# Query, key and value projections of a self-attention as three float32r products of split operands

## The chip, the core and the metric

One core of a Trainium2 chip runs the whole program. The metric is the device time of one execution in microseconds (us), the median of several. The engines have queues of their own and wait for each other by semaphores only: TensorE (PE in the rows; PEld is its weight load), VectorE (DVE), ScalarE (ACT), GpSimd (POOL), SyncE (SP, which issues the transfers).

## The reference

Inputs are x (2 x 1024 tokens, 256 features) and a context of 2 x 77 tokens. Two layers follow. The part that matters here is the start of the first one:

```python
h = layernorm(x)
ca = attention(q=h @ cq_w + cq_b, k=ctx @ ck_w + ck_b, v=ctx @ cv_w + cv_b)   # 16 heads of 16, 77 keys
x1 = norm(ca @ co_w + co_b + h) * co_g + co_be
q, k, v = x1 @ sq_w + sq_b, x1 @ sk_w + sk_b, x1 @ sv_w + sv_b                 # the change is here
sa = attention(q, k, v)                                                        # 1024 keys
...                                       # output norm, GELU block, experts, second attention, ternary block
```

## The kernel before

The 2048 tokens are 16 tiles of 128 (t), four tiles a block (k). The program has three parts. Part A (0 to about 215 us) does the first attention and the projections of the second. Part B (to about 565 us) is the self-attention over 32 batch-heads. Part C is everything else.

Part A is a list of steps, `ORDER_A`, written out by hand. Each engine walks the same list and does its share of each step, in that order and in no other: an instruction that waits holds up all later steps of its engine. Steps carry a tile, block or other number (S.13). They are:

- LS: moments of x on VectorE, reciprocal root on GpSimd (function `root`, L1919 and L1920). LN0: normalised tile (VectorE L1493), transposed (TensorE L861), copied by ScalarE (L1276). QP: queries of a block (TensorE L855).
- S: scores on TensorE (L908, L915), maximum and subtraction on VectorE (L1530, L1531). E: exponential on ScalarE. T: transposes of the probabilities in four groups, ScalarE copies each (L1298). PV: values (TensorE L931, ScalarE L1304). OT: transposes (TensorE L861 to OUT), divided on VectorE (L1538, L1539). CT: transposes again, ScalarE copies. PJ: output projection on TensorE (L855), residual addition and moments on VectorE (L1522, L1486, L1487), root on GpSimd. PN: normalisation of the projected tile on VectorE (L1493, L1496, L1497). RA: a bias addition on GpSimd (L1929).
- LT: transposes of the tile that PN wrote (TensorE L861, ScalarE L1276), into `xTb`. QK: query and key projections of a block, four groups `e` of 128 features by 512 tokens (TensorE L855). For each group ScalarE makes two copies (L1356, L1357), VectorE their difference (L1634), and SyncE stores both parts. SV: value projection of a tile (TensorE L855), bias addition on VectorE (L1640).
- MX: score maxima of the first two heads of part B (TensorE L962, VectorE L1555). MT, LH: maxima to rows, load of first heads. UT, GG, FL: a low-rank weight product for part C. FL is 4 products with 16 rows contracted, copied by ScalarE (L1343). KW, VV, MK, KB, V0, VW, CX, CK, ZS: preparation.

TensorE writes to rings of PSUM banks. `TR` has two banks, emptied by ScalarE; `OUT` has two banks, emptied by VectorE (OT, PJ, SV); the scores have their own four. A step that takes a bank waits until the user two before it in the same ring has been emptied:

```python
def out_bank(tl):
    bank = tl.slot(out_full, 2)
    tl.next(out_full)
    v = tl.back(out_full, 2)
    pe.wait_ge(out_done.sem, v)
    return OUT[:, bank, :]
```

All products of the projections are in float32; the trace shows each as two MATMUL instructions. Part B and the last stage of part C use float32r, one instruction a product. Part B begins on TensorE when every bank of part A is emptied, FL's among them. At the same point SyncE issues the loads of four weight arrays, and soon after the rows of head 1's maxima.

Of the kernel before, what the change touches and what calls it, by code (L numbers as in the profile page):

```python
# [23 lines left out]
F32 = mybir.dt.float32  # L24
# [9 lines left out]
KD = D // 128  # L34
# [57 lines left out]
    "LT": dict(tr=1),  # L92
    "RA": dict(res=1),
# [268 lines left out]
def build(nc, A, out):  # L362
    ctx = ExitStack()
    with ctx:
# [39 lines left out]
        projT = sb("projT", [128, MF, D], F32R)  # L404
        so, wq, wo = (sb(n, [128, KD, D]) for n in ("so", "wq", "wo"))
# [28 lines left out]
        xTb, xTs = xT3[:, 0], xT3[:, 1]  # L434

# [130 lines left out]
        placed = Signal(sem("slots_placed"), **count("place"))  # L566
        h_ready = Signal(sem("high_parts_ready"), **count("top"))
# [1513 lines left out]
```

## Time and profile before

| | us |
|---|---|
| median of 3 runs | 1096.81 |
| lowest, highest | 1096.51, 1098.58 |
| profiled execution, first to last instruction | 1094.8 |
| mean granted TensorE clock in it | 0.975 |
| TensorE matmul busy | 1019.2 |
| VectorE busy | 782.0 |
| ScalarE busy | 607.7 |
| GpSimd busy | 331.8 |

For the profiled execution the span is what the profile gives; its own time lies above the span by what comes before the first and after the last instruction. Matmuls are pipelined and their ends are modelled, so starts and distances of starts say more than durations. The granted clock is 1.00 at 2.4 GHz and 0.50 at 1.2 GHz.

### The profile page before, as it was taken

To read this page: it belongs to the slowest core of one execution; us is meant where nothing else is said; L and a number is where in the kernel's file an instruction comes from. 1 tells how busy PE (TensorE), PEld (TensorE's weight loads), DVE (VectorE), ACT (ScalarE), POOL (GpSimd) and SP (SyncE) were. 2 spreads that over 40 slices of the span, in tenths; PEclk is the share of its full clock that TensorE was granted. 3 is DMA by queue.
4 is the path that set the end of the run, shared out by engine and by line. 5 is a ranking of instruction groups with operands and counts; after the bars stand their busy time and mean duration, and the time that the engine had idled before them with its cause. 6 is when DMAs were issued, how large, how long until landed. Compare 5 with 4: busy or idle time off the path is not lost.

```text
span 1094.8 us, 20748 instructions
## 1 busy us (share of the span) xinstructions
PE 1019.2 (93%) x7648; PEld 601.0 (55%) x7648; DVE 782.0 (71%) x1337; ACT 607.7 (56%) x1191; POOL 331.8 (30%) x724
## 2 busy tenths in 40 slices
PE   5999989999999999999988898989898999999998
PEld 3675666433333333333344665648677676576865
DVE  4786577689999999999723747546536756887565
ACT  2665554478888888888853123131222456556543
POOL 3422111001010343344103334373366433530000
PEclk9999999889999999999998997999999999999999
DMA  7302221451221212212125100021344301100000
GB/s 213 70 16 88 87 68 66 144 188 44 75 71 48 70 49 69 79 45 70 47 67 191 34 15 10 20 77 44 101 155 132 100 31 49 44 25 1 16 18 26
DMA packets 97578, 75.67 MB, mean 69 GB/s; under 512 B 49806, under 2 KB 87483, under 8 KB 97223
## 3 DMA queue, kind: packets, MB, share of 16 engines
q1 hardware_dynamic: 94407, 65.95, 20.0%
q0 software_dynamic: 3072, 8.39, 2.4%
q8 instruction: 63, 1.03, 0.4%
q14 instruction: 36, 0.29, 0.1%
HBM read 42.94 MB, written 30.93 MB: 67 GB/s over the span
## 4 chain that ended last, share of the span: by engine, by line
PE 65%; DVE 10%; DMA 8%; issue 5%; POOL 4%; ACT 4%; SPq 3%; POOLq 0%; DVEq 0%; ACTq 0%
PE OUT L855 15%; PE TR L855 14%; PE OUT L1090 9%; PE TR L861 8%; PE TR L1079 7%; DMA head_q<-MT 7%; PE OUT L1079 3%; PE TR L931 3%; PE SCR L915 2%; POOL dispatched L2038 2%; SPq L697 2%; ACT PTS L1298 2%; PE SCR L908 2%; DVE small L1486 1%; PE OUT L861 1%
## 5 line engine op out<-in xcount | busy, mean ns | idle before, releaser
L1555 DVE TENSOR_REDUCE small<-SCR 128x1 f32<-128x1024 f32 x256 | 308.5, 1223 | 26.2 <-PE SCR L962 20.3
L1396 ACT ACTIVATE shared<-TR 128x512 f32<-128x512 f32 x352 | 200.1, 597 | 38.8 <-PE TR L1079 30.7
L962 PE MATMUL SCR<-head_k,head_q 48*128 48x512 f32 x512 | 193.9, 456 | 2.7 <-DVE P L1531 2.7
L1090 PE MATMUL OUT<-shared,HM 128*32 128x256 f32 x2048 | 165.3, 394 | 1.2 <-ACT shared L1396 0.4
L1079 PE MATMUL TR<-head_q,head_k 51*128 51x512 f32 x352 | 149.7, 463 | 0.9 <-issue 0.6
L1919 POOL TENSOR_SCALAR small<-small 128x1 f32<-128x1 f32 x112 | 27.7, 247 | 346.7 <-DVE small L1487 344.5
L855 PE MATMUL TR<-xT,fifo 128*128 128x512 f32 x224 | 105.8, 629 | 1.1 <-ACT xT L1276 1.0
L1396 ACT ACTIVATE shared<-OUT 128x512 f32<-128x512 f32 x160 | 95.8, 599 | 19.3 <-PE OUT L1079 17.6
L1079 PEld LDWEIGHTS TR<-head_q,head_k 51*128 51x128 f32 x352 | 60.6, 186 | 76.4 <-ACT shared L1396 56.5
L1276 ACT ACTIVATE xT<-TR 128x256 f32<-128x256 f32 x96 | 35.4, 381 | 111.5 <-PE TR L861 108.6
L1090 PEld LDWEIGHTS OUT<-shared,HM 128*32 128x32 f32 x2048 | 41.4, 108 | 93.1 <-ACT shared L1396 57.6
L1298 ACT ACTIVATE PTS<-TR 96x512 f32<-96x512 f32 x128 | 69.6, 589 | 38.5 <-PE TR L861 37.8
L1936 POOL CAST small<-small 128x8 bf16<-128x8 f32 x32 | 6.1, 190 | 256.5 <-DVE small L1555 256.5
L962 PEld LDWEIGHTS SCR<-head_k,head_q 48*128 48x128 f32 x512 | 79.1, 187 | 7.0 <-DVE P L1531 3.0
L861 PE MATMUL TR<-identf,P 128*96 128x128 f32 x512 | 71.1, 281 | 7.7 <-ACT PTS L1298 7.4
L855 PEld LDWEIGHTS TR<-xT,fifo 128*128 128x128 f32 x224 | 44.4, 203 | 55.3 <-issue 49.1
L1079 PE MATMUL OUT<-head_q,head_k 51*128 51x512 f32 x160 | 70.2, 438 | 4.7 <-DMA head_q<-MT 4.2
L1920 POOL TENSOR_TENSOR small<-small 128x1 f32<-128x1 f32 x112 | 67.1, 599 | 9.3
L861 PEld LDWEIGHTS TR<-identf,P 128*96 128x96 f32 x512 | 52.8, 127 | 23.4 <-ACT PTS L1298 16.3
L1530 DVE TENSOR_REDUCE small<-SCR 128x16 f32<-128x1232 f32 (+1 forms) x32 | 48.7, 1522 | 20.2 <-PE SCR L915 19.9
L855 PE MATMUL OUT<-fifo,shared 128*128 128x256 f32 x256 | 58.2, 382 | 2.0 <-ACT shared L1426 1.6
L855 PE MATMUL TR<-xT,fcT 128*128 128x512 f32 x128 | 56.2, 595 | 1.0 <-ACT RR L1440 1.0
(241 smaller groups left out, 1860.3 us busy)
## 6 DMA issues: line engine op xcount, KB each, us to landing
pieces<-pieces SPq DMA_DIRECT2D x16, 512.0 KB, 2.7
HM<-dispatched SPq DMA_DIRECT2D x46, 128.0 KB
expert_out<-HM SPq DMA_DIRECT2D x46, 128.0 KB
dispatched<-HB SPq DMA_DIRECT2D x6, 768.0 KB, 4.0
head_q<-pieces SPq DMA_DIRECT2D x32, 128.0 KB
head_k<-pieces SPq DMA_DIRECT2D x32, 128.0 KB
shared<-in_L_ffn_w SPq DMA_DIRECT2D x4, 1024.0 KB, 12.0
x<-TOK SPq DMA_DIRECT2D x16, 128.0 KB, 1.7
```

Source lines behind the costliest of these rows:

```text
L855: ins = nc.tensor.matmul(dst, l, r, start=(n == 0), stop=(n == len(pairs) - 1))
L861: ins = nc.tensor.transpose(dst[0:m, n * width:n * width + p], s, ident[0:p, 0:p])
L931: ins = nc.tensor.matmul(bank[32 * g:32 * g + 32, c * 128:(c + 1) * 128], VSW[0:KP, h, :], PTS[0:KP, place, :], start=True, stop=True)
L962: ins = nc.tensor.matmul(SQ[kt % 2][:, hf, :], QX[n % 2][rows, kt * 128:(kt + 1) * 128], KX[n % 2][rows, hf * 512:(hf + 1) * 512], start=T ...
L1079: nc.tensor.matmul(bank, KX[n % 2][rows, kt * 128:(kt + 1) * 128], QX[n % 2][rows, hf * 512:(hf + 1) * 512], start=True, stop=True)\
L1090: ins = nc.tensor.matmul(PV[32 * g:32 * g + 32, 0:256], VH[:, n % 2, kt, :], PTB[:, kt % 2, g * 256:(g + 1) * 256], start=(kt == 0), stop= ...
L1276: nc.scalar.activation(dst[:, :, c:c + 128], bank[:, 0:256].rearrange("p (k n) -> p k n", k=KD), ACT.Copy)\
L1298: nc.scalar.activation(PTS[0:KP, 4 * g:4 * g + 4, :], bank[0:KP].rearrange("p (h n) -> p h n", h=4), ACT.Copy)\
L1396: nc.scalar.activation(PTB[:, kt % 2, hf * 512:(hf + 1) * 512], ring_bank("t_scores", n, kt, hf), ACT.Exp, scale=DH ** -0.5).then_inc(st_d ...
L1530: chain(nc.vector.tensor_reduce(mx, v, AX, ALU.max))
L1555: nc.vector.tensor_reduce(nm[:, n % 2, kt:kt + 1], SQ[kt % 2].rearrange("p h n -> p (h n)"), AX, ALU.max, negate=True).then_inc(sq_done.se ...
L1920: nc.gpsimd.tensor_tensor(rstd[:, r:r + 1], ve[:, r:r + 1], minus_half, ALU.pow)\
```

## The change

The input of the self-attention projections, x1, and the three weights are each split in a high part (rounded to float32r) and a low part (the rest, as float32r). A product becomes three: high by high, high by low, low by high, accumulated in one bank. QK has six float32r products a group in place of two float32 ones, and SV likewise.

Step LT becomes LA: the transposes go to an OUT bank, ScalarE copies it into `XAH` (high part), and VectorE subtracts that from the same bank into `XAL` and frees the bank. QK and SV wait for VectorE's part of LA. A new step WS on GpSimd splits the weights once, before QP.1. FL moves from between MX.1.6 and MX.1.7 to the very end of the list. PN of a tile waits for LA's transposes of the tile two before it, where it waited for LT's copy; VectorE's own part of LA stands ahead of it in the list.

```diff
     "LT": dict(tr=1),
+    "LA": dict(out=1, ahi=1),
+    "WS": dict(),
...
-QP.1 PV.2 LN0.8 LS.10 LS.9 LS.12 S.4 LS.11 T.3 E.4 OT.2 PJ.1 PV.3 S.5 CT.2 OT.3 T.4 PJ.2 LT.0 PV.4 RA.6 RA.3 E.5 PN.1
-CT.3 LS.13 S.6 OT.4 T.5 PN.2 PJ.3 LT.1 E.6 PV.5 CT.4 S.7 T.6 OT.5 SV.1 E.7 LT.2 PV.6 RA.4 LN0.10 PN.3 PJ.4 CT.5 OT.6
-T.7 LS.14 LN0.11 LN0.9 RA.5 SV.0 RA.7 LT.3 PV.7 LN0.12 RA.8 RA.10 VW.1 PJ.5 CT.6 RA.12 QP.2 LN0.13 SV.2 PN.5 S.8 QK.0
-S.9 E.8 OT.7 PN.4 SV.3 T.8 S.10 E.9 PV.8 PJ.6 LT.4 CT.7 OT.8 T.9 E.10 PJ.7 SV.4 CT.8 PV.9 LN0.14 PN.6 PJ.8 LT.5 LT.6
-PN.7 OT.9 T.10 RA.9 SV.5 LT.7 PV.10 LN0.15 SV.7 CT.9 QK.1 S.11 LH.0 QP.3 PJ.9 E.11 OT.10 S.12 T.11 SV.6 E.12 PN.8 S.13
-PN.9 CT.10 PV.11 LT.8 PJ.10 OT.11 T.12 S.14 CT.11 RA.11 E.13 PN.10 PV.12 PJ.11 RA.13 T.13 E.14 OT.12 S.15 CT.12 MX.0.0
-LT.10 LH.1 E.15 PV.13 PJ.12 LT.9 MX.0.1 SV.10 RA.14 MX.0.2 T.14 OT.13 MX.0.3 MX.0.4 PV.14 CT.13 MX.0.5 PN.11 RA.15
-SV.9 MX.0.6 T.15 OT.14 MX.0.7 PJ.13 LT.11 PN.12 PV.15 PN.13 MX.1.0 CT.14 MX.1.1 OT.15 PJ.14 QK.2 SV.11 CT.15 SV.8
-LT.12 PN.14 MT PJ.15 LT.13 MX.1.2 UT PN.15 SV.12 LT.14 SV.13 MX.1.3 MX.1.4 LT.15 SV.14 QK.3 MX.1.5 MX.1.6 FL MX.1.7
-SV.15
...
+WS QP.1 PV.2 LN0.8 LS.10 LS.9 LS.12 S.4 LS.11 T.3 E.4 OT.2 PJ.1 PV.3 S.5 CT.2 OT.3 T.4 PJ.2 LA.0 PV.4 RA.6 RA.3 E.5
+PN.1 CT.3 LS.13 S.6 OT.4 T.5 PN.2 PJ.3 LA.1 E.6 PV.5 CT.4 S.7 T.6 OT.5 SV.1 E.7 LA.2 PV.6 RA.4 LN0.10 PN.3 PJ.4 CT.5
+OT.6 T.7 LS.14 LN0.11 LN0.9 RA.5 SV.0 RA.7 LA.3 PV.7 LN0.12 RA.8 RA.10 VW.1 PJ.5 CT.6 RA.12 QP.2 LN0.13 SV.2 PN.5 S.8
+QK.0 S.9 E.8 OT.7 PN.4 SV.3 T.8 S.10 E.9 PV.8 PJ.6 LA.4 CT.7 OT.8 T.9 E.10 PJ.7 SV.4 CT.8 PV.9 LN0.14 PN.6 PJ.8 LA.5
+LA.6 PN.7 OT.9 T.10 RA.9 SV.5 LA.7 PV.10 LN0.15 SV.7 CT.9 QK.1 S.11 LH.0 QP.3 PJ.9 E.11 OT.10 S.12 T.11 SV.6 E.12 PN.8
+S.13 PN.9 CT.10 PV.11 LA.8 PJ.10 OT.11 T.12 S.14 CT.11 RA.11 E.13 PN.10 PV.12 PJ.11 RA.13 T.13 E.14 OT.12 S.15 CT.12
+MX.0.0 LA.10 LH.1 E.15 PV.13 PJ.12 LA.9 MX.0.1 SV.10 RA.14 MX.0.2 T.14 OT.13 MX.0.3 MX.0.4 PV.14 CT.13 MX.0.5 PN.11
+RA.15 SV.9 MX.0.6 T.15 OT.14 MX.0.7 PJ.13 LA.11 PN.12 PV.15 PN.13 MX.1.0 CT.14 MX.1.1 OT.15 PJ.14 QK.2 SV.11 CT.15
+SV.8 LA.12 PN.14 MT PJ.15 LA.13 MX.1.2 UT PN.15 SV.12 LA.14 SV.13 MX.1.3 MX.1.4 LA.15 SV.14 QK.3 MX.1.5 MX.1.6 MX.1.7
+SV.15 FL
...
-            before(("LT", t), ("PN", t + 2))
+            before((last, t), ("PN", t + 2))
...
-    attention_order(before, range(T))
+    attention_order(before, range(T), "LA")
+    before(("WS",), ("LA", 0))
     for t in range(T):
         k = t // BT
         for u in range((k - 1) * BT, k * BT):
             if u >= 0:
-                before(("SV", u), ("LT", t))
+                before(("SV", u), ("LA", t))
         if k >= 1:
-            before(("QK", k - 1), ("LT", t))
+            before(("QK", k - 1), ("LA", t))
...
+        WH = over("self_weights_high", [128, 3, KD, D], F32R, "projT")
+        WL = over("self_weights_low", [128, 3, KD, D], F32R, "fifo", 1024)
...
+        XAH, XAL = (over(f"self_in_{n}", [128, KD, N], F32R, "xT3", KD * N * j) for j, n in enumerate(("high", "low")))
...
+            def self_input(t):
+                pe.wait_ge(tok_ready.sem, tl.after(tok_ready, "PN", t))
+                bank = out_bank(tl)
+                transposes(bank, [TOK[:, t % 2, k * 128:(k + 1) * 128] for k in range(KD)]).then_inc(out_full.sem, 1)
+
             def self_qk(k):
-                at.block_copied("LT", k)
-                for w in (sq, sk):
-                    for m in range(KD):
-                        at.feature_major(w, xTb, m)
+                pe.wait_ge(out_done.sem, tl.after_block(out_done, "LA", k))
+                pe.wait_ge(ws_ready, 1)
+                for e in range(2 * KD):
+                    j, c = e // KD, slice(e % KD * 128, e % KD * 128 + 128)
+                    bank = tr_bank(tl)
+                    product(bank, [(w[:, j, f, c], x[:, f, :]) for f in range(KD)
+                                   for w, x in ((WH, XAH), (WH, XAL), (WL, XAH))]).then_inc(tr_full.sem, 1)
 
             def self_values(t):
-                at.copied("LT", t)
-                at.token_major(xTb, sv, t, range(KD))
+                pe.wait_ge(out_done.sem, tl.after(out_done, "LA", t))
+                pe.wait_ge(ws_ready, 1)
+                bank = out_bank(tl)
+                c = slice(t % BT * 128, t % BT * 128 + 128)
+                product(bank[:, 0:D], [(x[:, f, c], w[:, 2, f, :]) for f in range(KD)
+                                       for x, w in ((XAH, WH), (XAH, WL), (XAL, WH))]).then_inc(out_full.sem, 1)
...
+            def self_input(t):
+                bank = OUT[:, tl.slot(out_full, 2), :]
+                act.wait_ge(out_full.sem, tl.next(out_full))
+                c = t % BT * 128
+                nc.scalar.activation(XAH[:, :, c:c + 128], bank[:, 0:256].rearrange("p (k n) -> p k n", k=KD), ACT.Copy)\
+                    .then_inc(xa_ready.sem, 1)
...
-                    left(tl, "LT", t - 2)
+                    dve.wait_ge(out_full.sem, tl.after(out_full, "LA", t - 2))
                 normalised(tl, chain, ("PJ", t), HB[:, t % 2, :], TOK[:, t % 2, :], affine="co")\
                     .then_inc(tok_ready.sem, 1)
+
+            def self_input(t):
+
+                bank = filled(tl)
+                dve.wait_ge(xa_ready.sem, tl.next(xa_ready))
+                c = t % BT * 128
+                signal_out(tl, nc.vector.tensor_tensor(
+                    XAL[:, :, c:c + 128], bank[:, 0:256].rearrange("p (k n) -> p k n", k=KD),
+                    XAH[:, :, c:c + 128].bitcast(F32), ALU.subtract))
...
+            def self_weights():
+
+                pool.wait_ge(d_aw, 16 * 4)
+                for j, w in enumerate((sq, sk, sv)):
+                    chain(nc.gpsimd.tensor_copy(WH[:, j, :, :], w))
+                    ins = nc.gpsimd.tensor_tensor(WL[:, j, :, :], w, WH[:, j, :, :].bitcast(F32), ALU.subtract)
+                ins.then_inc(ws_ready, 1)
```

## Rows read from the trace of the kernel before

**Rows 1.** Page, part 1: busy us (share of the span) and instructions.
```profile
PE 1019.2 (93%) x7648; PEld 601.0 (55%) x7648; DVE 782.0 (71%) x1337; ACT 607.7 (56%) x1191; POOL 331.8 (30%) x724
```

**Rows 2.** Windows view, 50 to 200 us: length, busy of each engine, clock, DMA.
```profile
50.00:200.00 150.00, 142.86 (x1253) 97.64 (x1252) 112.76 (x208) 83.75 (x149) 28.90 (x62) 0.99 0.19 68
```

**Rows 3.** Chain of work in order of time: start, us, what.
```profile
91.91 0.87 PE OUT L855 x4
...
124.03 6.87 PE TR L855 x16
...
197.62 1.13 PE SCR L962 x4
...
222.68 6.46 DMA head_q<-MT
...
232.24 0.23 PE TR L1079
```

**Rows 4.** Timeline of PE, output stage, float32r: start, us, engine, line.
```profile
1087.05 0.28 PE L855 MATMUL OUT<-projT,hidL 128*128 128x256 f32 x1
1087.17 0.28 PE L855 MATMUL OUT<-projT,hidH 128*128 128x256 f32 x1
```

**Rows 5.** Timeline of ACT in QK.0: one copy of a group.
```profile
97.73 0.69 ACT L1356 ACTIVATE pieces<-TR,sq_b 128x512 fp32r<-128x512 f32 x1 [0.32 <-PE TR L855]
```

**Rows 6.** Groups by line, 0 to 300 us: an OUT bank through DVE.
```profile
L1640 DVE TENSOR_TENSOR shared<-OUT,rows_a 128x256 f32<-128x256 f32 x16 | 6.7, 421 | 9.3 <-PE OUT L855 9.2
```

**Rows 7.** Timelines at OT.11: PE's OT.11, then the end of DVE's PN.9.
```profile
145.49 0.60 PE L861 MATMUL OUT<-identf,OSB 128*128 128x128 f32 x4
...
147.12 0.42 DVE L1497 TENSOR_TENSOR TOK<-TOK,rows_a 128x256 f32<-128x256 f32 x1
```

**Rows 8.** Timelines at OT.8: PE's OT.8, then DVE's PJ.6.
```profile
110.16 0.60 PE L861 MATMUL OUT<-identf,OSB 128*128 128x128 f32 x4
...
111.41 0.41 DVE L1522 TENSOR_TENSOR HB<-OUT,XN 128x256 f32<-128x256 f32 x1
```

**Rows 9.** Timelines at OT.9: PE's OT.9, then the end of DVE's PJ.8.
```profile
117.55 0.60 PE L861 MATMUL OUT<-identf,OSB 128*128 128x128 f32 x4
...
118.23 0.18 DVE L1487 BATCH_NORM_AGGREGATE small<-small 128x2 f32<-128x6 f32 x1
```

**Rows 10.** Timelines, end of part A: QK.2's last piece, MX, QK.3, FL, part B.
```profile
191.42 0.69 DVE L1634 TENSOR_TENSOR pieces<-RR,pieces 128x512 fp32r<-128x512 f32 x1 [1.02 <-ACT RR L1357]
...
198.67 2.36 DVE L1555 TENSOR_REDUCE small<-SCR 128x1 f32<-128x1024 f32 x2
...
199.82 7.03 PE L855 MATMUL TR<-xT,fifo 128*128 128x512 f32 x16
...
207.91 3.82 PE L855 MATMUL TR<-MW 16*128 16x512 f32 x8
...
215.44 0.76 PE L1079 MATMUL TR<-head_q,head_k 51*128 51x512 f32 x1 [0.56 <-issue]
```

**Rows 11.** Timelines and groups of POOL and of DVE beside it.
```profile
53.08 0.57 POOL L1920 TENSOR_TENSOR small<-small 128x1 f32<-128x1 f32 x1
...
65.85 0.40 DVE L1493 TENSOR_SCALAR TOK<-HB,small 128x256 f32<-128x256 f32 x1
...
83.75 2.78 POOL L1929 TENSOR_TENSOR XN<-XN,rows_a 128x256 f32<-128x256 f32 x4
...
85.76 0.92 DVE L1493 TENSOR_SCALAR XN<-X,small 128x256 f32<-128x256 f32 x1
...
L1974 POOL COPY HM<-shared 128x136 f32<-128x136 f32 x32 | 9.7, 305 | 3.1 <-PE OUT L1090 1.2 <-DVE shared L1640 0.3
```

**Rows 12.** PE's wait for S.15, and windows of PE after it and after FL.
```profile
159.14 0.73 PE L962 MATMUL SCR<-head_k,head_q 48*128 48x512 f32 x2 [2.74 <-DVE P L1531]
...
160.00:164.00 4.00, 4.00 (x40) 0.57 0.14 50
...
212.00:214.00 2.00, 2.00 (x5) 0.50 0.00 0
```

More of the change, by code:

```diff
@@ L179, with attention_order @@
 """
-def attention_order(before, tiles):
+def attention_order(before, tiles, last="LT"):
     for t in tiles[:-1]:
@@ L566, in build @@
         placed = Signal(sem("slots_placed"), **count("place"))
+        xa_ready = Signal(sem("self_in_high_ready"), **count("ahi"))
         h_ready = Signal(sem("high_parts_ready"), **count("top"))
@@ L570, in build @@
                   "pc": (pc_ready,), "gate": (gate_exp,), "act": (a_ready,), "low": (l_ready,),
-                  "pick": (picked,), "place": (placed,)}
+                  "pick": (picked,), "place": (placed,), "ahi": (xa_ready,)}
         d_rb = [sem(f"residual_loaded_{r}") for r in range(BT)]
@@ L596, in build @@
         wscale_ready = sem("weight_scales_ready")
+        ws_ready = sem("self_weights_split")
         tern_ready = Signal(sem("ternary_ready"), b=(1 + KD) * MF)
@@ L1063, in _ @@
                 "LN0": lambda t: at.transposed(XN[:, t % TB, :], ("LN0", t)),
-                "QP": queries, "QK": self_qk, "SV": self_values, "MX": first_maxima})
+                "QP": queries, "LA": self_input, "QK": self_qk, "SV": self_values, "MX": first_maxima})
             tl0.close(sq_full)
@@ L1361, in _ @@
                 "KW": lambda: small_keys(kT1, cols["bk"], d_l1, 4), "UT": low_rank_transposes, "GG": low_rank_middle,
-                "FL": low_rank_product, "LN0": lambda t: copy_transposed(tl, xT2[:, t // BT % 2], t), "QK": self_qk,
+                "FL": low_rank_product, "LN0": lambda t: copy_transposed(tl, xT2[:, t // BT % 2], t), "LA": self_input, "QK": self_qk,
                 "MT": first_maxima_rows})
@@ L1647, in _ @@
                 "PJ": lambda t: with_residual(tl, chain, t, HB[:, t % 2, :], XN[:, t % TB, :], "RA"),
-                "PN": projected_norm, "QK": pieces, "SV": self_values, "MX": lambda n, kt: max_scores(tl0, n, kt)})
+                "PN": projected_norm, "LA": self_input, "QK": pieces, "SV": self_values, "MX": lambda n, kt: max_scores(tl0, n, kt)})
             tl0.close(sq_full)
@@ L1942, in _ @@
             tl0, tl = Tally("b0"), Tally("a")
-            chain = Chain(0, ln_stats.per["a"] + 2 * 3)
+            chain = Chain(0, ln_stats.per["a"] + 2 * 3 + 3)
             def first_maxima(n, kt):
@@ L1967, in bias_a @@
                 add_bias(XN[:, t % TB, :], "co_b")
-            tl.walk(order_a, groups, roots(tl, chain) | {"KW": layer_1_keys, "RA": bias_a, "MX": first_maxima})
+            tl.walk(order_a, groups, roots(tl, chain) | {"KW": layer_1_keys, "WS": self_weights, "RA": bias_a, "MX": first_maxima})
             chain.close(1)
```

## The prediction

> **What bounds the kernel now.** I read the page first: TensorE is busy 93% of the span and VectorE 71% [rows 1]. The change touches only part A (up to about 215 us) and its hand-over to part B, so the windows view comes next: from 50 to 200 us, the body of part A, TensorE is busy 142.9 of 150 us, VectorE 112.8, ScalarE 83.8, GpSimd 28.9 [rows 2]. The chain in order of time then says who releases whom: nearly every piece is TensorE following TensorE. A QK block takes 6.87 us of it, four times over; a value product (SV) 0.87 [rows 3]. So part A is a TensorE queue in which seconds saved are seconds gained, as long as nobody else becomes late. Who is nearly late is the second question, and the instruction timelines of VectorE answer it: in several places VectorE works without a pause and several steps behind TensorE [rows 7, 8, 9, 10].
>
> **What it removes.** A float32 product of 128x512 columns is two instructions in the trace, so QK is 16 of them: 6.87/16 = 0.43 us each. A float32r product is one: 128x256 ones start every 0.12 us in the output stage, and 128x512 ones advance the chain by 0.23 [rows 4]. After the change one of the four groups is 6 x 0.23 = 1.4 us in place of 1.72, a QK block 5.5 in place of 6.9. The upper bound for a 512-column float32r product is 0.28, from four of them on the chain (1.13/4), by which QK takes 6.8 and nothing is won. I take 0.23, since twice 0.12 agrees. ScalarE's two copies per group are 0.69 us each [rows 5], 1.4 at most; it would follow, not bound. Four blocks: 4 x 1.4 = 5.6. An SV is 6 x 0.12 = 0.72 in place of 0.87; 16 of them: 2.4. Together 8.0 us of TensorE time.
>
> **What it adds.** (1) Sixteen VectorE subtractions out of PSUM, 128x256: 0.42 like the SV row, 0.45 from start to start [rows 6]; 7.2 us on an engine that is 71% busy. The ScalarE copy stays (0.38). (2) GpSimd's weight split WS, three copies and three subtractions of 128x512. Four bias additions of 128x256 take 2.78, so one of 512 columns at most 1.4; a copy of 136 columns is 305 ns, so one of 512 lies between 0.65 (half of the 305 being fixed) and the addition's 1.4. Sum 6.2 to 8.4 us [rows 11]. In its queue WS stands after the root of LS.15, which ends at 53.65, and before five roots (LS.10, 9, 12, 11 and PJ.1) of 0.85: PJ.1's would end between 64.1 and 66.3. PN.1 wants it at 65.85 [rows 11], or 66.3 behind LA.0. So I take 0. The cover is the time that PJ.1's root lies ready now; with it gone, PN.1 holds up the whole queue of VectorE behind it.
>
> GpSimd also slows VectorE where they meet. One normalisation of 128x256 that began at 85.76, while the four bias additions ran until 86.53, took 0.92; PN.1's of the same shape took 0.40 [rows 11]. The Trainium skill ("SBUF — State Buffer", Who interferes with whom) has the rule: a VectorE scalar operation in its two-port mode, or one with two SBUF inputs, waits until the GpSimd instruction ends. The trace agrees. By the rule WS would cost one instruction's rest wherever a PN or LN0 falls between 53.6 and 62.1; none does, so it leaves the sum alone.
>
> (3) The transposed input now passes through the OUT ring (two banks, drained by VectorE in its own queue order) and not TR. This is where I see the loss: TensorE may take an OUT bank only when the user two before it is drained, and LA is drained only when VectorE comes to it. I walk the order with the timelines, times as before:
>
> - Start, LA.1 to LN0.12: LA.1 needs OT.4 drained, which is only just in time now and comes later by LA.0's subtraction: 0.5. LN0.10's and LN0.12's normalisations stand behind LA.2 and LA.3: 0.45 and 0.5. Together 1.4.
> - OT.8 (110.16) is second after PJ.6, whose addition on VectorE ends at 111.82 behind the two passes of S.10: TensorE waits 1.5 [rows 8].
> - OT.9 (117.55) is second after LA.5; VectorE does PJ.8 until 118.4, then LA.5 until 118.8: 1.1, and LN0.15 behind LA.7: 0.5 [rows 9].
> - OT.11 (145.49) is second after LA.8. VectorE is in S.13 and PN.9 until 147.54 and in LA.8 until 147.95: TensorE waits 2.3, and T.12, S.14 and S.15 stand behind it in its queue [rows 7].
>
> Before QK.2 that is 1.4 + 1.5 + 1.6 + 2.3 = 6.8 given back against two QK blocks (2.8) and some eight SVs on the path (1.2): +2.8 us. LA.10, 9 and 11 meet VectorE idle or banks long empty: nothing.
>
> (4) The end. VectorE works without a pause from the last piece of QK.2 (ends 192.1) to MX.1.4 (201.03), and QK.3 starts at 199.82 because LT.15 asked only ScalarE [rows 10]. Now QK.2's last piece ends 1.0 earlier (not 1.4: VectorE enters that block late), but LA.12 to LA.15 add 4 x 0.45, a wait of 0.3 for LA.12 comes in, and QK.3 must wait for LA.15, behind MX.1.4: 191.1 + 8.9 + 1.8 + 0.3 = 202.1, so +2.2. After that QK.3 wins 1.2. FL (3.82 us [rows 10]) stood between MX.1.6 and MX.1.7, in VectorE's shadow; now TensorE idles some 2 us there and does FL last, with ScalarE's last copy behind, while part B waits for it. From QK.3's start to B's was 15.6 us (199.82 to 215.44). It becomes 5.5 for QK.3, 1.1 for MX.1.5 and 1.6, 2.3 idle until VectorE has emptied MX.1.5's banks, 0.7 for MX.1.7, 0.7 for SV.15, 3.4 for FL and 0.7 for the last copy (as in [rows 5]): 14.4 at full clock. So B starts 2.2 - 1.2 = 1.0 later, relative to QK.2; with FL at half clock, 6.9 us, 4.5 later. The granted clock was 0.50 from 212 to 214, right after FL, and 0.57 from 160 to 164, after TensorE had waited 2.7 us for S.15 [rows 12] (the two levels are 2.4 and 1.2 GHz); so I expect part of FL at 1.2 GHz and take +2.5, near the middle between 1.0 and 4.5. The rule of the Trainium skill ("TensorE: Matmul & The Clock Gate", HAM oscillation) that idle gaps bring the half clock back points the same way; these numbers rest on the rows.
>
> Part B keeps its pace: after its start the path goes through the transfer of head 1's maxima, which lands behind the weight loads that are issued at that same start (6.46 us on the chain) [rows 3], so a later start shifts everything rigidly. The edit's other parts (semaphores, overlays) cost nothing that I can find: the high weights lie in a tile that is written only after part B.
>
> **Sum.** 2.8 + 2.5 = +5.3. The profiled span is 1094.8; 2.0 lie between it and the median of 1096.81, and I let them stand: 1100.1 + 2.0 = 1102.1 us, 0.5% slower. 0.2% (2.2 us) is about what a measurement of this kernel can tell from no change.
>
> **Rivals.**
> - *The stalls as costed*, the forecast: 1099.5 to 1104.5. Chance 0.44.
> - *The half clock comes twice.* The 2.3 us wait at OT.11 is like the 2.7 us for S.15, after which 4 us ran at 0.57 [rows 12]: 4 x 0.43 = +1.7; with all of FL cold: 2.8 + 1.7 + 4.5 = +9.0, 1105.8. For it: both triggers have a precedent. Against: neither repeats exactly. 0.14.
> - *Banks are found empty* (the other side). If OT.8, OT.9 and OT.11 find their banks drained, because my mapping of steps to rows is off by one user, 4.9 falls away, QK.3's wait for LA.15 stays: 5.3 - 4.9 = +0.4; with the early lags (1.4 + 0.5) absorbed too and FL at full clock (1.5) it is -3.0, and at most -8.0 + 1.0 = -7.0: 1090 to 1094. It decides at OT.11: above 1 us of waiting there it is dead. For it: VectorE is 30% idle on average. Against: its idle time lies elsewhere. 0.17.
> - *Even.* The three ring stalls are there, but the early lags are taken up before QK.0 and FL runs warm: 2.8 - 1.9 + 1.0 = +1.9, 1098.7. Or float32r at 0.28 with shorter stalls. 0.19.
> - *GpSimd late.* If a float32r output doubles WS to 12 to 16 us, PN.1 and all of VectorE's queue wait 5 to 8 us: +10 or more, 1107. For it: no GpSimd row writes float32r. Against: VectorE's and ScalarE's rows that write it cost no more than float32. 0.06.
>
> Faster by over 0.2% 0.17, within 0.19, slower 0.64. The range goes from the other side's gentler half, 1091, to the late GpSimd, 1107; outside lie the extreme of the third rival and of the last. The likeliest case's own range is 1099.5 to 1104.5.
>
> **What the next profile would show.** QK groups of about 5.5 us between first and last product (right) or 6.8 (float32r no faster); OT.11 released by VectorE's LA.8 with over 1 us of TensorE idle; QK.3 released by LA.15's subtraction and not by ScalarE; ScalarE's FL copies last before part B; a granted clock below 1 near there; WS about 6 to 9 us and PN.1 not waiting for GpSimd. The prediction is wrong if TensorE's idle time in part A does not grow by about 8 us, or if the clock's half-rate stretches in parts B and C move by chance by more than that.

## The result, and the profile after

The changed kernel takes 1117.15 us (median of four runs, 1110.11 to 1131.75; one of them is left out of the ratio) where the kernel before takes 1096.66 on the same chip: ratio 1.0165, interval 1.0122 to 1.0209. A second comparison further down gives 1.0184 (1.0145 to 1.0223). Slower was right; 1102.1 us and the range up to 1107 were not. The loss is 18 to 20 us instead of 5.3.

The profiled execution took 1117.78 us, its span is 1115.8 (before: 1094.8). The page's part 1, the answer to [rows 1]:

```profile
PE 1028.8 (92%) x7712; PEld 612.9 (55%) x7712; DVE 789.9 (71%) x1353; ACT 608.6 (55%) x1191; POOL 336.8 (30%) x730
```

TensorE has 64 more matmuls and 9.6 us more busy time, although each new product is shorter. That is a first sign of the clock: work at 1.2 GHz is busy for longer (FL 7.13 us here, 3.75 on the chain before). The windows view (length, busy time of each engine, granted clock, DMA share, GB/s), against [rows 2]:

```profile
50.00:200.00 150.00, 134.68 (x1270) 98.01 (x1268) 111.63 (x209) 82.20 (x145) 34.14 (x67) 0.98 0.18 64
200.00:215.00 15.00, 12.48 (x48) 9.12 (x47) 9.36 (x19) 2.78 (x6) 0.79 (x2) 0.69 0.13 48
215.00:230.00 15.00, 12.71 (x34) 7.33 (x33) 7.04 (x9) 5.65 (x10) 1.75 (x8) 0.73 0.37 140
230.00:300.00 70.00, 67.49 (x521) 24.60 (x523) 52.59 (x51) 49.83 (x104) 5.43 (x25) 0.81 0.31 100
```

In the same 150 us TensorE is busy 8.2 us less (134.7 against 142.9). It stands still, and the view of waits says for whom. Its columns: who waited <- for whom, us in total, times, longest; TensorE from 60 to 228 us of the changed kernel, without two lines for ScalarE's PTS (3.2 and 0.3 us) that the kernel before has too (3.2 and 0.2):

```profile
...
PE OUT L869 <- DVE self_in_low L1662: 2.8, 2, 2.2
PE SCR L970 <- DVE P L1558: 2.7, 1, 2.7
PE OUT L863 <- DVE shared L1676: 2.4, 1, 2.4
PE SCR L970 <- DVE small L1582: 2.3, 1, 2.3
PE OUT L869 <- DVE HB L1549: 2.0, 2, 1.6
PE TR L869 <- DVE XN L1520: 1.4, 3, 0.5
PE OUT L869 <- DVE CA L1566: 1.1, 2, 0.8
PE OUT L869 <- DVE shared L1676: 1.0, 1, 1.0
```

The 2.7 us for S.15's P stood there before [rows 12]. Nearly all the rest is new (the kernel before has 0.2 us for XN and one wait of 0.4 at an OUT bank, for ScalarE). Every line shown ends at VectorE; five of the eight are OUT banks. The 2.3 us for `small` are MX.1.7's, where FL no longer stands. The stalls at OT.8 and OT.11, to be read against [rows 8] and [rows 7], are in PE's timeline (start, us, engine, line, what, and in brackets the idle time before it with its releaser):

```profile
113.48 0.63 PE L869 MATMUL OUT<-identf,OSB 128*128 128x128 f32 x4 [1.65 <-DVE HB L1549]
...
151.67 0.63 PE L869 MATMUL OUT<-identf,OSB 128*128 128x128 f32 x4 [2.21 <-DVE self_in_low L1662]
...
205.81 0.55 PE L863 MATMUL OUT<-self_weights_high,self_in_high 128*128 128x256 f32 x1 [2.42 <-DVE shared L1676]
...
222.92 1.22 PE L970 MATMUL SCR<-head_k,head_q 48*128 48x512 f32 x2 [2.29 <-DVE small L1582]
...
233.52 0.79 PE L1099 MATMUL TR<-head_q,head_k 51*128 51x512 f32 x1 [0.69 <-ACT fcT L1363]
```

VectorE's timeline beside the second of them shows the mechanism. The subtraction LA.8 stands behind the passes of S.13 and the three of PN.9, and TensorE's OT.11 starts when it ends:

```profile
148.51 1.44 DVE L1558 TENSOR_TENSOR P<-SCR,small 128x1232 f32<-128x1232 f32 x1
149.87 0.41 DVE L1520 TENSOR_SCALAR TOK<-HB,small 128x256 f32<-128x256 f32 x1
150.31 0.42 DVE L1523 TENSOR_TENSOR TOK<-TOK,rows_a 128x256 f32<-128x256 f32 x1
150.76 0.42 DVE L1524 TENSOR_TENSOR TOK<-TOK,rows_a 128x256 f32<-128x256 f32 x1
151.11 0.42 DVE L1662 TENSOR_TENSOR self_in_low<-OUT,self_in_high 128x256 fp32r<-128x256 f32 x1
```

The end of part A on the chain in order of time, against [rows 10] and [rows 3]:

```profile
205.81 1.62 PE OUT L863 x6
...
211.43 8.09 PE TR L863 x24
221.64 1.24 DVE small L1582
222.92 1.22 PE SCR L970 x2
224.13 1.58 PE OUT L863 x6
225.71 7.13 PE TR L863 x8
...
240.80 7.89 DMA head_q<-MT
```

QK.3 takes 8.09 us here, where QK.1 took 5.9 at full clock: its first ten products start 0.43 us apart and the rest 0.23. FL takes 7.13 us instead of 3.8 [rows 10]. SV.15 takes 1.58, where 0.7 was forecast; in the kernel before it took 2.00 and MX.1.7 1.15, for there the clock had fallen by then too (0.50 from 212 to 214 [rows 12]). The chain of the kernel before:

```profile
211.73 1.15 PE SCR L962 x2
212.88 2.00 PE OUT L855 x4
```

No step has more work than forecast; the clock is at 1.2 GHz. Part B starts at 233.52 and not at 215.44.

GpSimd's WS, against [rows 11], one of its three pairs and the root that follows the last:

```profile
54.21 0.61 POOL L2002 CAST self_weights_high<-fifo 128x512 fp32r<-128x512 f32 x1
54.90 1.27 POOL L2003 TENSOR_TENSOR self_weights_low<-fifo,self_weights_high 128x512 fp32r<-128x512 f32 x1
...
59.95 0.24 POOL L1955 TENSOR_SCALAR small<-small 128x1 f32<-128x1 f32 x1
```

### The profile page after: what moved, and what is told of

It reads as the page before. It is cut to its first block, busy times and chain, and to the rows that moved or that the text cites. A ratio compares the mean times of both kernels' runs of the same rounds, so it can differ in the third digit from the quotient of the medians.

```text
span 1115.8 us, 20921 instructions
## 1 busy us (share of the span) xinstructions
PE 1028.8 (92%) x7712; PEld 612.9 (55%) x7712; DVE 789.9 (71%) x1353; ACT 608.6 (55%) x1191; POOL 336.8 (30%) x730
## 4 chain that ended last, share of the span: by engine, by line
PE 65%; DVE 14%; DMA 7%; issue 5%; ACT 4%; POOL 3%; SPq 1%; DVEq 0%; POOLq 0%; ACTq 0%
PE TR L863 16%; PE OUT L863 12%; PE OUT L1110 10%; PE TR L1099 8%; PE TR L869 7%; DMA head_q<-MT 5%; PE OUT L1099 4%; PE TR L939 2%; DVE small L1557 2%; PE SCR L923 2%; DVE small L1513 2%; PE OUT L869 1%; ACT PTS L1318 1%; PE SCR L916 1%; SPq L705 1%
## 5 line engine op out<-in xcount | busy, mean ns | idle before, releaser
L970 PE MATMUL SCR<-head_k,head_q 48*128 48x512 f32 x512 | 198.1, 465 | 5.0 <-DVE P L1558 2.7
L1110 PE MATMUL OUT<-shared,HM 128*32 128x256 f32 x2048 | 167.9, 400 | 1.2 <-ACT shared L1423 0.4
L1296 ACT ACTIVATE xT<-TR 128x256 f32<-128x256 f32 x80 | 29.4, 382 | 95.0 <-PE TR L869 94.4
L863 PE MATMUL TR<-xT,fifo 128*128 128x512 f32 x160 | 79.0, 654 | 1.3 <-ACT xT L1296 1.0
L863 PEld LDWEIGHTS TR<-xT,fifo 128*128 128x128 f32 x160 | 33.1, 212 | 42.4 <-issue 40.3
## 6 DMA issues: line engine op xcount, KB each, us to landing
shared<-in_L_ffn_w SPq DMA_DIRECT2D x4, 1024.0 KB, 11.4
```

The costliest lines, as they stand in the source:

```text
L863: ins = nc.tensor.matmul(dst, l, r, start=(n == 0), stop=(n == len(pairs) - 1))
L970: ins = nc.tensor.matmul(SQ[kt % 2][:, hf, :], QX[n % 2][rows, kt * 128:(kt + 1) * 128], KX[n % 2][rows, hf * 512:(hf + 1) * 512], start=T ...
L1110: ins = nc.tensor.matmul(PV[32 * g:32 * g + 32, 0:256], VH[:, n % 2, kt, :], PTB[:, kt % 2, g * 256:(g + 1) * 256], start=(kt == 0), stop= ...
L1296: nc.scalar.activation(dst[:, :, c:c + 128], bank[:, 0:256].rearrange("p (k n) -> p k n", k=KD), ACT.Copy)\
```

## The experiments

Every ratio is to the kernel before, run beside it. To compare traces I use three marks of TensorE's timeline: S.4's mask products (53.31 us before, 53.91 after), MX.0.0 (159.14, 165.35) and the first product of part B (215.44, 233.52). Counting from S.4 removes what the start of the program adds by chance (it lay between 52.0 and 56.7 us). The clock is the mean granted clock from 150 to 300 us.

| kernel | ratio (interval) | S.4 to MX.0.0 | S.4 to part B | clock |
|---|---|---|---|---|
| before; again (e10) | 1; one look | 105.8; 105.8 | 162.1; 162.2 | 0.94; 0.94 |
| changed; again (e13) | 1.0165; 1.0184 (1.0145 to 1.0223) | 111.4; 111.4 | 179.6; 177.2 | 0.83; 0.82 |
| e1, e14: changed, FL back | 1.0171 (1.0129 to 1.0213); 1.0155 (1.0119 to 1.0191) | 112.6; 111.4 | 176.4; 175.2 | 0.86; 0.87 |
| e2: before, FL at the end | 1.0062 (1.0035 to 1.0089) | 105.8 | 167.2 | 0.93 |
| e3: changed, float32 products | 1.0203 (1.0182 to 1.0224) | 115.4 | 183.6 | 0.90 |
| e4: changed, LA in TR | 1.0111 (1.0085 to 1.0137) | 106.7 | 174.9 | 0.85 |
| e5: e4, FL back | 1.0084 (1.0052 to 1.0115) | 106.5 | 170.0 | 0.87 |
| e6: e5, GpSimd subtracts | 1.0006 (0.9978 to 1.0034) | 104.2 | 164.3 | 0.76 |
| e8: e6, UT and FL early | 1.0061 (1.0028 to 1.0094) | 108.7 | 165.6 | 0.83 |
| e7; e11: e5 without low part of input | 0.9999 (0.9972 to 1.0027); one look | 102.9; 102.9 | 161.9; 161.8 | 0.89; 0.84 |
| e9: before, 16 subtractions | 1.0054 (1.0028 to 1.0080) | 106.7 | 168.8 | 0.84 |
| e12: split in tiles 0 to 7 only | 0.9989 (0.9963 to 1.0015) | 104.2 | 161.4 | 0.92 |
| e15: before, one copy in OUT | 1.0156 (1.0122 to 1.0189) | 113.3 | 175.3 | 0.93 |

The last three columns come from one profiled execution each. Those of e6, e8 and e9 took 1118.22, 1114.45 and 1110.11 us where their medians are 1100.65, 1107.67 and 1101.85; those of e2, e12, e14 and e15 are the shortest of their runs. Their part B marks and clocks stand for that one execution only.

**The clock over all runs.** The granted clock and the span are on record for every run, so the time at half clock can be worked out for each: 2 x (1 - clock) x span. Over the 78 runs of the kernel before that stood beside the experiments, span and half clock go together: 0.41 us of span for each us at half clock (correlation 0.92, each comparison taken by itself; the other kernels' own runs give 0.35). With 0.41 a kernel's loss splits in a share of the clock and a rest. This split is an estimate, good to 1 or 2 us. In us, means of the runs that the ratio uses, less those of the kernel before beside them:

| kernel | span | time at half clock | the clock's share | rest |
|---|---|---|---|---|
| changed (e13) | +20.1 | +21.7 | +8.9 | +11.2 |
| e14: changed, FL back | +15.3 | +14.5 | +6.0 | +9.4 |
| e2: before, FL at the end | +6.2 | +8.2 | +3.4 | +2.8 |
| e3: changed, float32 products | +22.1 | +12.1 | +5.0 | +17.1 |
| e4: changed, LA in TR | +11.4 | +16.3 | +6.7 | +4.7 |
| e5: e4, FL back | +8.5 | +14.1 | +5.8 | +2.7 |
| e6: e5, GpSimd subtracts | +0.9 | +2.6 | +1.1 | -0.2 |
| e8: e6, UT and FL early | +7.0 | +18.4 | +7.6 | -0.5 |
| e7: e5 without low part of input | -0.4 | +10.9 | +4.5 | -4.9 |
| e9: before, 16 subtractions | +5.5 | +12.0 | +4.9 | +0.6 |
| e12: split in tiles 0 to 7 only | -0.6 | +1.9 | +0.8 | -1.4 |
| e15: before, one copy in OUT | +16.1 | +6.3 | +2.6 | +13.6 |

**FL's place, e1 and e2.** In ORDER_A of the changed kernel:

```
-MX.1.5 MX.1.6 MX.1.7 SV.15 FL
+MX.1.5 MX.1.6 FL MX.1.7 SV.15
```

> The changed kernel with one step moved: the low-rank product FL goes back between MX.1.6 and MX.1.7, where it stood before. The computation is unchanged. Theory: part of the loss is that FL at the end (7.19 us for eight 16-row products, all at half clock) stands between the last products of part A and the first of part B; put back, part B starts some 5 us earlier, so about 1112 us (ratio 1.012 to 1.014). Rival 1, the loss lies in the ring stalls and in what VectorE does alone: FL costs the same wherever it stands, and the time stays within 1.5 us of 1117. Rival 2, the longer half-clock stretch at the start of part B comes from FL: then 8 us or more come back, 1109 or less.

And the reverse edit, in the kernel before:

> The kernel before with that one step moved and nothing else: FL goes from between MX.1.6 and MX.1.7 to the very end, after SV.15. The computation is unchanged. Theory: FL at the end costs 3 to 6 us by itself (1100 to 1103 us). Rival: in the kernel before, FL delays MX.1.7 and so the first head of part B, and moving it costs nothing or gains up to 2 us (1095 to 1097).

Alone, the move costs 0.62% (some 6.8 us; 5.1 of them are there when part B starts), at or a little above the upper end of the theory's 3 to 6. In the changed kernel moving it back gave nothing that this measurement can tell, against the theory of e1.

**The products, e3.** In QK, and likewise in SV (ScalarE's copy of LA then goes to `xTb`, and the low weights lie in another spare buffer):

```
-product(bank, [(w[:, j, f, c], x[:, f, :]) for f in range(KD)
-               for w, x in ((WH, XAH), (WH, XAL), (WL, XAH))])
+product(bank, [((sq, sk)[j][:, f, c], xTb[:, f, :]) for f in range(KD)])
```

> The changed kernel with the products of QK and SV as they were before (two float32 products for each bank, on the unsplit weights and the transposed tile), while LA keeps its place in the OUT ring, ScalarE's copy and VectorE's subtraction (here of equal numbers), GpSimd keeps the splitting of the weights, and FL stays at the end. Theory: the float32r products are the only gain of the change; without them QK takes 1 to 1.4 us longer each and SV 0.15 us each, so the time is 3 to 6 us above the changed kernel, 1120 to 1123. Rival: the products are covered by ScalarE's emptying of the banks and by VectorE, and the time stays within 2 us of 1117.

1.0203 against 1.0165 and 1.0184: the float32r products are worth some 0.2 to 0.4% in this kernel, 2 to 4 us, and the intervals overlap. They do not pay for the rest. With the clock taken out they are worth more, about 6 us (rest 17.1 against 11.2): the changed kernel has 10 us more at half clock.

**The ring, e4.** LA's bank comes from TR. ScalarE empties it twice, VectorE subtracts in SBUF, and QK and SV wait for `xa_ready`:

```
-"LA": dict(out=1, ahi=1),
+"LA": dict(tr=1, ahi=1),
 ScalarE:  activation(XAH[...], bank, Copy)
+          activation(TOKM[:, t % 2, :], bank, Copy)   -> tr_done
-VectorE:  XAL = bank - XAH                            -> out_done
+VectorE:  XAL = TOKM[:, t % 2, :] - XAH               -> xa_ready
```

> The changed kernel with LA's transposes in the TR ring, which ScalarE empties, as LT's were before: ScalarE copies the bank twice, once rounded to the high part and once in full to a spare buffer, and frees it; VectorE subtracts from the spare buffer, in SBUF, and PE waits for the low part only before QK and SV. float32r products and FL at the end stay. Theory: the OUT-ring stalls on PE (0.83, 1.65, 2.21, 2.42 us and smaller ones, about 9 us by QK.3) go, ScalarE gains 16 copies of 0.69 us; the time falls to 1108 to 1112. Rival: it is the subtraction's own time on VectorE and not the ring that makes part A longer, and the time stays within 3 us of 1117. Rival 2: ScalarE's second copies cost as much as the ring, above 1117.

As expected: 1.0111, and MX.0.0 comes 4.7 us sooner after S.4, with 16 more copies on ScalarE. The OUT-ring stalls on LA and OT are gone from the view of waits; waits for the low part (2.1 us at a QK block, 0.4 at SVs) have come in.

**What is left, e5 to e8.** e5 is e4 with FL back:

> Both repairs together: LA in the TR ring (ScalarE's two copies, VectorE's subtraction from SBUF) and FL back between MX.1.6 and MX.1.7. The full computation. The TR ring alone took the ratio to the kernel before from 1.017 to 1.011, FL at the end alone cost 1.006 on the kernel before. Theory, the two losses add: ratio 1.005, some 1101 to 1103 us where the kernel before has 1096. Rival: they cover the same wait at the end of part A, and the ratio stays at 1.009 to 1.012.

1.0084, between theory and rival and not told apart by the ratio; the trace has part B 4.9 us earlier. e6 moves the subtraction to GpSimd:

```
-nc.vector.tensor_tensor(XAL[...], TOKM[...], XAH[...], ALU.subtract)
+nc.gpsimd.tensor_tensor(XAL[...], TOKM[...], XAH[...], ALU.subtract)
```

> As the kernel with LA in the TR ring and FL back, but GpSimd does the 16 subtractions instead of VectorE, which then does nothing that it did not do before the change. The full computation. Theory: what the ring leaves of the loss is VectorE's 16 times 0.4 us, so this one lies 2 to 5 us below its neighbour with the subtraction on VectorE, at a ratio of 1.000 to 1.003. Rival: the subtraction on VectorE lies in its idle time and moving it changes less than 1.5 us, or GpSimd's slower subtraction (about 0.65 us each, half of the 1.27 us of a 512-column one) delays the norms' roots and shared memory access on VectorE, and it is slower.

1.0006: 0.8% came back, no less than the 6.7 us (0.6%) that 16 operations of 0.42 us take if each counts in full, although GpSimd needs 0.73 us for each. By the split above, 2.9 us of it are the rest and 4.7 the clock's share, so the 6.7 us are not VectorE's time counted in full. e8 also moves UT and FL into the wait for S.15:

```
-S.15 CT.12 MX.0.0            -MX.1.2 UT PN.15            -MX.1.6 FL MX.1.7
+S.15 CT.12 UT FL MX.0.0      +MX.1.2 PN.15               +MX.1.6 MX.1.7
```

> As the kernel with GpSimd's subtraction, but UT and FL stand before MX.0.0, where PE waits 2.7 us for VectorE's scores of S.15 in every kernel so far. The full computation. Theory: FL's 3.8 to 5 us of eight products and copies take the place of that idle time, and part B no longer starts behind them: 2 to 4 us below the neighbour with FL between MX.1.6 and MX.1.7, ratio 0.997 to 1.000. Rival: PE idles at the end of part A for VectorE anyway (2.3 us before MX.1.7), so FL there was half hidden too, and the gain is under 1 us; or ScalarE's eight copies delay the exponentials of tile 15 and it is slower.

It missed: 1.0061. In the profiles UT and FL cost 4.5 us before MX.0.0 (108.7 against 104.2), where the idle time was 2.7, and the 2.3 us wait for VectorE before MX.1.7 is back, since nothing fills it. Yet part B starts only 1.3 us later, and by the split e8 and e6 have the same rest; their whole difference of 6 us is the clock's share. Why e8 has 16 us more at half clock is not shown. e7 has TensorE's part alone:

```
-... for w, x in ((WH, XAH), (WH, XAL), (WL, XAH))]
+... for w, x in ((WH, XAH), (WH, XAH), (WL, XAH))]
```

> PE's part of the change alone: the six float32r products for each bank and GpSimd's splitting of the weights stay, but LA's transposes go through the TR ring with the one copy by ScalarE (rounded to the high part), there is no subtraction by any engine, the high part of the input stands in for the low part, so that the low part of the input is left out of the computation, and FL is back in its place. Theory: this is what the faster products are worth with nothing against them: 4 times 1.0 to 1.4 us and 16 times 0.15 us, of which the half hidden behind ScalarE's emptying is lost, so a ratio of 0.994 to 0.997 (3 to 6 us faster than before). Rival: the products were hidden behind ScalarE and VectorE all along, ratio 0.998 to 1.002. Rival 2: GpSimd's splitting costs something that the trace does not show, above 1.002.

The first rival won: 0.9999. Yet MX.0.0 is reached 2.9 us sooner, so the products were not hidden. The gain is lost afterwards. The windows of TensorE behind the wait for S.15 and to the end of part A (length, PE busy, granted clock, DMA share, GB/s), first of this kernel:

```profile
157.00:172.00 15.00, 15.00 (x106) 0.57 0.08 29
172.00:205.00 33.00, 32.05 (x201) 1.00 0.28 102
205.00:245.00 40.00, 38.02 (x242) 0.74 0.50 176
```

and of the kernel before in its first profile:

```profile
157.00:172.00 15.00, 12.62 (x109) 0.89 0.14 48
172.00:205.00 33.00, 32.37 (x160) 1.00 0.24 88
205.00:245.00 40.00, 39.21 (x260) 0.83 0.56 193
```

After the same 2.5 to 2.7 us of idle time TensorE runs at 1.2 GHz for about 13 of 15 us in one kernel and for 3.4 in the other. QK.2 then starts at 183.3 in the one and at 183.0 in the other, 130.3 and 129.7 us after S.4: the lead of 2.9 us is gone. The 11 runs of e7 say the same as its profile: the products are worth some 4.9 us, and 4.5 go to the clock.

**Is that chance? e10 and e11**, both kernels once more:

> The kernel before once more, unchanged, for a second profile of it. Question: how long PE runs at the half clock behind the wait for tile 15's scores (3.4 us in the first profile, at 160 to 163 us) and at the start of part B (13.65 us). Theory of chance: these lengths differ from one execution to the next, and this one shows others. Rival: they are the same again, and the 12 us at 158 to 170 us of the kernel with the float32r products are that kernel's own.

> The kernel with PE's part of the change alone once more, unchanged (float32r products, LA through the TR ring with one copy, no subtraction, the low part of the input left out), for a second profile of it. Theory of chance: the half clock behind the wait for tile 15's scores lasts another time than the 12 us of the first profile, and where it is shorter, QK.2 starts up to 3 us before its time in the kernel before. Rival: 12 us again.

Not chance from one execution to the next. The kernel before again:

```profile
157.00:172.00 15.00, 12.29 (x108) 0.89 0.16 52
205.00:245.00 40.00, 38.94 (x257) 0.83 0.56 194
```

The products alone again:

```profile
157.00:172.00 15.00, 15.00 (x96) 0.59 0.06 25
205.00:245.00 40.00, 39.44 (x204) 0.57 0.41 146
```

The first stretch repeats in both; the one around part B's start repeats in the kernel before (0.83) and differs in the other (0.74, 0.57).

**VectorE's time alone, e9.** At each LT step of the kernel before:

```
+nc.vector.tensor_tensor(TOKM[:, t % 2, :], X[:, t, :], X[:, (t + 1) % T, :], ALU.subtract)
```

> The kernel before with one thing added: at each LT step VectorE does a subtraction of 256 columns (two tiles of the input, into a spare buffer that nothing reads), without any wait. The computation is unchanged. Theory: VectorE's 16 times 0.4 us are the subtraction's price, since VectorE sets the pace at the end of part A; 2 to 7 us slower, ratio 1.002 to 1.006 (moving the subtraction from VectorE to GpSimd gave back 0.8 per cent). Rival: on the kernel before VectorE has 25 per cent idle time, and the ratio stays under 1.002, so that what GpSimd gave back was a wait and not VectorE's time.

1.0054, in the theory's upper part, but not by the theory's way. By the split VectorE's time is worth 0.6 us and the clock 4.9, so the number came out right by luck. The profiled execution shows where, and overstates it, for it took 8 us more than the median: MX.0.0 is only 0.8 us late, part B 6.7. In between the clock did this:

```profile
157.00:172.00 15.00, 12.26 (x75) 0.63 0.16 54
205.00:245.00 40.00, 39.44 (x162) 0.63 0.46 164
```

This kernel has float32 products throughout, so long half-clock stretches are not the float32r products' own.

**A better version? e12** splits the first batch only; LA.8 to LA.15 become LT steps with float32 products:

```
-MX.0.0 LA.10 LH.1 E.15 PV.13 PJ.12 LA.9
+MX.0.0 LT.10 LH.1 E.15 PV.13 PJ.12 LT.9
+if k >= BLOCKS: float32 products of sq, sk on xTb
```

> The split for the first batch only: tiles 0 to 7 (QK.0, QK.1, SV.0 to SV.7) as in the kernel with the TR ring, ScalarE's two copies and GpSimd's subtraction; tiles 8 to 15 with one copy and float32 products, as before the change; FL in its old place. The full computation. Theory: part A reaches MX.0.0 some 2 us earlier than before, as in the kernels with GpSimd's subtraction, and its end is that of the kernel before, without the 0.8, 0.7 and 0.6 us waits for the low parts; ratio 0.996 to 0.999. Rival: the end of part A is set by VectorE, or the half clock takes what is gained, and the ratio is 0.999 to 1.003.

0.9989 (0.9963 to 1.0015): the fastest of all, not told apart from the kernel before.

**FL's share and the ring by itself: e13, e14, e15.** The changed kernel and e1 side by side:

> The changed kernel unchanged, beside its neighbour with FL back in its old place, on the same chip: the first comparison had three and six runs and left FL's share of the loss open. Expected: ratio 1.015 to 1.020 to the kernel before.

> The changed kernel with FL back between MX.1.6 and MX.1.7, beside the changed kernel itself. Theory: FL's move is worth what it was in two other kernels (0.6 per cent from the kernel before, 0.3 per cent in the TR ring), so this is 0.3 to 0.6 per cent below the changed kernel. Rival: in the changed kernel VectorE holds PE up at the end of part A wherever FL stands (2.3 us idle before MX.1.7), and the two are within 0.2 per cent.

1.0184 and 1.0155: 0.3% apart, the edge of the theory, with overlapping intervals. With the first pair (no difference) FL's share in the changed kernel is somewhere between nothing and about 0.6%; this stays open. e15 puts the ring into the kernel before, with VectorE doing ScalarE's copy:

```
-"LT": dict(tr=1)      ScalarE:  xTb = bank  -> tr_done
+"LA": dict(out=1)     VectorE:  xTb = bank  -> out_done
```

> The kernel before with one thing changed: the transposes of the self-attention's input go to an OUT bank, and VectorE copies it (one copy of 256 columns, no subtraction, no copy by ScalarE); float32 products, FL in its old place. The full computation. Theory: the price of 16 subtractions on VectorE without a ring was 0.54 per cent, and taking LA out of the OUT ring gave the changed kernel 0.5 to 0.6 per cent back; together the ratio is 1.009 to 1.013, and MX.0.0 starts 5 to 7 us later than in the kernel before. Rival: without ScalarE's copy ahead of VectorE the bank is free 0.7 us earlier, most ring stalls go, and the ratio is that of the 16 operations alone, 1.004 to 1.007.

1.0156, more than the theory had: nearly the whole loss of the change, without float32r, split, ScalarE copy or FL's move. Its view of waits, TensorE from 60 to 228 us, has nearly the stalls of the changed kernel (a ScalarE copy ahead of VectorE is not what they need). MX.0.0 comes 7.5 us late. And here the clock is not the cause: 13.6 of its 16.1 us are rest.

```profile
...
PE OUT L862 <- DVE xT L1639: 2.9, 2, 2.4
...
PE OUT L862 <- DVE HB L1528: 2.0, 2, 1.7
PE OUT L856 <- DVE shared L1651: 2.0, 1, 2.0
PE OUT L862 <- DVE CA L1545: 0.8, 1, 0.8
PE OUT L862 <- DVE shared L1651: 0.8, 1, 0.8
```

## Why the prediction was wrong in size

The direction and the ring mechanism held. The step that failed is (4), The end: it added 2.5 us from MX.0.0 to part B where 9.5 to 11.9 were measured, since it left out two stalls and put nearly all of that stretch at full clock. The gain of the products was mis-sized too. In the terms of the split, the forecast of +5.3 was 3.8 of stalls and work and 1.5 of clock; measured are 11.2 and 8.9.

- **Stalls up to MX.0.0: right.** Predicted 6.8 us; the timeline lists 0.83, 0.29, 0.47, 0.47, 1.65, 0.39, 0.59, 0.47 and 2.21, together 7.4, less the 0.6 that the kernel before had there. OT.8 (1.5 predicted, 1.65 measured), OT.11 (2.3, 2.21) and OT.9 with LA.6 (1.1, 0.98) stand where the walk put them, released by the instructions that it named. "Banks are found empty" is dead by its own test, 1 us at OT.11. e4 and e15 show the cause: out of the ring the stalls are gone; with the ring alone they are all there.
- **The gain up to MX.0.0: too large.** Two QK blocks and eight SVs were to give 4.0 us; e7 shows 2.9 (between e3 and the changed kernel it is 4.0, with 3.4 us of half clock of e3 before MX.0.0 in it). A float32r product does take 0.23 us, but before the third group of a block the starts lie 0.41 to 0.48 us apart, since the bank must first be emptied and ScalarE needs two copies of 0.69, so a block takes 5.9 us and not 5.5. MX.0.0 came 5.6 us late and not some 3. e15, which has the stalls and float32 products, is 7.5 late there: so the stalls with their small gaps cost about 7.5 and the products gave back only 1.9.
- **The end: the step that failed.** From MX.0.0 to part B the prediction added 2.5 us; the two profiles of the changed kernel add 11.9 and 9.5. First, the ring: behind OT.11 I costed one stall, 0.3 us for LA.12. LA.12 waits 1.05, and SV.13 waits 2.42 for SV.12's bank, which VectorE drains behind PN.15. QK.3 is released by LA.15's subtraction, as forecast, but starts 21.6 us after QK.2 and not 19.0 (202.1 less 199.82 is 2.3, by the way, and not 2.2). Second, the clock: from QK.3 to part B my list of pieces is complete, but it has them at full clock except for FL: 14.4 us, 17.9 at worst. Measured were 8.0 for QK.3, 1.2, 2.3 idle, 1.2, 1.6, 7.2 and 0.7, in all 22.1. I also took the 15.6 us of the kernel before for a figure at full clock, though MX.1.7 and SV.15 are in it at half clock (1.15 and 2.00 us, where the list has 0.7 each). The price of a late bank was its wait; here there is also the clock behind it. e9 shows that price by itself, 4.9 us where next to nothing was late; e15 shows that it need not come, 2.6 us behind the same stalls.
- **FL last** was a true cost, 0.62% alone, where the pieces of step (4) that belong to it make 2.6 us (2.3 idle, 0.7 for the copy, FL itself 0.4 shorter) and 6.1 with FL at half clock; e2 has 5.1 at part B's start. The changed kernel's part B starts 2.0 us sooner with FL back (e13, e14); how much of that it feels at the end is open, see above.
- **GpSimd's WS: right.** 5.8 us between 54.2 and 60.0 (6.2 to 8.4 predicted, so a little less), PJ.1's root by 64.2 and PN.1 at 66.89 behind LA.0, not behind GpSimd. e7 has WS too and is no slower than before.
- **VectorE's load** was costed only where it met a stall. Moving the subtraction to GpSimd gave back 0.8% (e5 to e6), more than half of it by the clock.
- **"The half clock comes twice"** was near in kind, but not in place or price: 9.0 us in all where 18 to 20 were lost. Its trigger, OT.11's wait of 2.21 us, brought no half clock in either profile of the changed kernel, though the same wait did in e1. TensorE from 150 to 154 us (length, PE busy, granted clock, DMA share, GB/s), the changed kernel and then e1:

```profile
150.00:154.00 4.00, 2.08 (x17) 1.00 0.22 81
...
150.00:154.00 4.00, 2.98 (x16) 0.67 0.22 82
```

  The half clock came elsewhere: 6.8 us in place of 3.4 behind the wait for S.15 (0.77 and 0.89 from 157 to 172 us), then behind SV.13's 2.42 us and MX.1.7's 2.29, and in long stretches after part B's start (0.81 from 230 to 300 us, where the kernel before has 1.00).
- **Rigid after part B's start: about right.** Part B starts 18.1 us later, the span is 21.0 longer; over the other kernels the two differ by 4 us less to 8 us more, by what the clock does after part B's start (in the long executions of e6 and e8 by 19 and 14).

What is shown: the main cause is that VectorE, in its own queue order, now empties LA's OUT bank. That alone costs 1.56% on the kernel before (e15), where 16 VectorE operations that nothing waits for cost 0.54% (e9), so about 1% is the ring's if the two add. Taken out of the changed kernel, the ring gives back 0.5 to 0.7% (e4) and the subtraction on VectorE another 0.8% (e5 to e6). The faster products return 0.2 to 0.4%, within the noise. The second cause is time at half clock, an estimated 9 of the 20 us. What sets it off and how long it lasts is not shown: e7 and e11 agree with each other (13 us behind the wait for S.15), e9 refutes that it is the float32r products, and e12 (7 us) and e5 (14) differ for no reason that I can name. Only FL was tried as a filling for that wait, and it gained nothing (e8).

## What to carry to other kernels

Before an operand is moved to another buffer ring, ask which engine empties that ring and what stands ahead in its queue at every user, to the last one and not only in the middle: here two banks behind a busy VectorE cost 0.5 to 1% where the faster products gave 0.2 to 0.4%. Where TensorE's clock has two levels, a stall can have a second price behind it (4.9 us in e9, 2.6 in e15); cost everything up to the next steady stretch at both levels, and compare the clock over all runs, not in one profile. And a product that takes 20% less time, on a kernel whose TensorE is 93% busy, can still be worth nothing (e7: 2.9 us won by MX.0.0 and lost again by QK.2, at the half clock), so measure it alone before paying for it with work on other engines.

## What the runs showed of the hardware

- A float32r product of 128x512 columns starts 0.23 us after the one before it, one of 256 columns 0.12, and 0.43 and 0.21 at the half clock (211.43 to 224.9 us): float32r at 1.2 GHz takes as long as each of a float32 product's two instructions at full clock.
- GpSimd's float32r copy of 128x512 took 0.61 us and its subtraction 1.27. Its 128x256 subtraction to float32r took 0.73 (e6), no more than its float32 additions of that size in the same trace (0.73 to 0.76), and VectorE's took 0.42 (e5).
- The length of the half clock behind a 2.7 us wait repeated from one execution to the next in one and the same kernel (0.89 and 0.89; 0.57 and 0.59 over 157 to 172 us) and was another in kernels whose work ahead of it had moved by 1 to 3 us (0.63 in e9).
- In the kernel before, executions with more time at half clock were longer by 0.41 us for each us of it (78 runs, granted clock 0.963 to 0.978).
